# The expert stage's last normalization on other engines, its quads in one step, and one tile less

## The reference

```
h = layernorm(x) * (1 + ca) + sa
x = x + ga * attention(h)                  # 16 heads, band of 32
h = layernorm(x) * (1 + cb) + sb
y = layernorm(h + mha(h)) * g1 + be1       # 4 heads, over the 16 sequences
e = argmax(y @ Wg.T)                       # one of 8 experts per row
z = layernorm(y + relu(y @ W1[e] + b1[e]) @ W2[e] + b2[e]) * g2 + be2
out = x + gb * z
```

## Time and profile before

| What | us |
|---|---|
| median of the three timed runs | 1231.72 |
| the three runs | 1231.72, 1223.13, 1233.21 |
| profiled execution | 1211.88 |
| its span | 1210.1 |

### The profile page before, as it was taken

One profiled execution on the slowest core, in us unless ns is written; L12 is line 12 of the kernel. 1 busy time (PEld: TensorE's weight loads), 2 busy tenths in 40 slices (PEclk: granted clock), 3 DMA queues, 4 the chain that ended last, 5 costly groups with the idle time before them and its releaser, 6 DMA issues. The chain is left out here.

```text
span 1210.1 us, 51704 instructions
## 1 busy us (share of the span) xinstructions
PE 1081.4 (89%) x18513; PEld 871.2 (72%) x18513; DVE 947.0 (78%) x4152; ACT 921.3 (76%) x3404; POOL 871.5 (72%) x732
## 2 busy tenths in 40 slices
PE   4799999999999999999999999489888887788994
PEld 2578778787777778787787777258676666677883
DVE  6888888888888888888888877358775664676775
ACT  3699999999999999999999989358664644355552
POOL 2788888888888888888888857354664666555667
PEclk9899999999999999999999999789877877899998
DMA  6776777777777776776777766351331117456100
GB/s 198 205 183 172 185 172 178 186 183 179 178 177 169 182 174 170 189 181 168 185 181 175 172 172 150 92 167 41 113 105 60 56 68 207 157 166 178 54 28 30
DMA packets 111037, 181.03 MB, mean 150 GB/s; under 512 B 19726, under 2 KB 64177, under 8 KB 110656
## 3 DMA queue, kind: packets, MB, share of 16 engines
q1 hardware_dynamic: 103520, 159.32, 51.8%
q0 software_dynamic: 6400, 16.82, 3.8%
q10 hardware_dynamic: 864, 1.57, 0.5%
HBM read 35.20 MB, written 24.73 MB: 50 GB/s over the span
## 5 line engine op out<-in xcount | busy, mean ns | idle before, releaser
L621 POOL TENSOR_TENSOR qk<-mm,sw 128x1024 f32<-128x1024 f32 x128 | 305.4, 2386 | 94.6 <-DMA sw<-mm 94.4
L692 ACT ACTIVATE pr<-sm,mn 128x96 f32<-128x96 f32 x1024 | 368.4, 369 | 0.3 <-DVE mn L522 0.3
L503 DVE TENSOR_TENSOR mm<-bank,cos 128x512 f32<-128x512 f32 x256 | 175.0, 684 | 75.4 <-PE bank L325 60.6
L627 POOL TENSOR_TENSOR pr<-pr,ri 128x768 f32<-128x768 f32 x128 | 188.8, 1475 | 30.3 <-DVE ri L531 29.7
L692 ACT ACTIVATION_READ_ACCUMULATOR pr<-sm,mn 128x1 f32 x1024 | 200.4, 196 | 0.0
L522 DVE CUSTOM_DVE_ANT_0 sm<-bank,msk 128x96 f32<-128x96 f32 x1024 | 190.9, 251 | 1.7 <-PE bank L337 1.6
L504 DVE TENSOR_TENSOR mm<-bank,sin 128x512 f32<-128x512 f32 x256 | 173.9, 679 | 0.0
L702 ACT ACTIVATE pT<-bank 96x512 f32<-96x512 f32 x256 | 136.9, 585 | 16.1 <-PE bank L352 14.2
L368 PE MATMUL bank<-pT,vw 96*64 96x64 f32 x4096 | 148.9, 226 | 0.0
L1263 ACT ACTIVATE fv<-bank,b1t 128x128 f32<-128x128 f32 x288 | 81.6, 375 | 84.5 <-PE bank L1096 64.5
L368 PEld LDWEIGHTS bank<-pT,vw 96*64 96x64 f32 x4096 | 131.1, 139 | 10.2 <-issue 0.7
(11 more groups left out here) (220 smaller groups left out, 2516.7 us busy)
## 6 DMA issues: line engine op xcount, KB each, us to landing
sw<-mm SPq DMA_DIRECT2D x512, 128.0 KB, 2.4
vw<-vn SPq DMA_DIRECT2D x128, 192.0 KB, 2.6
vw<-vn SPq DMA_DIRECT2D x128, 128.0 KB, 2.4
rr<-sorted_scratch SPq DMA_DIRECT2D x72, 192.5 KB
vw<-vn SPq DMA_DIRECT2D x96, 64.0 KB, 2.6
xt<-in_x SPq DMA_DIRECT2D x16, 256.0 KB, 4.7
x_scratch<-x SPq DMA_DIRECT2D x16, 256.0 KB, 2.7
rr<-x_scratch SPq DMA_DIRECT2D x16, 256.0 KB, 3.1
```

What stands on the lines that cost most here:

```text
L503: dve.tensor_tensor(mm[s % 2][:, 0, j, :], PJ[u % 2][:, :], cos[:, :], ALU.mult)
L621: pool.tensor_tensor(qk[i % 2][:, :, 32:], mm[i % 2][:, 0, :, :], sw[i % 2][:, :, :], ALU.add)\
L627: pool.tensor_tensor(t, t, ri[i % 2][:, :].unsqueeze(2).to_broadcast([P, 8, WK]), ALU.mult)\
L692: ins = act.activation(pr[i % 2][:, h, p, :], ms_[i % 2][:, h, p, :], ACT.Exp, scale=-1.0, bias=mn[i % 2][:, h, p:p + 1], accum_out=sums[i ...
```

## The change

Third stage only.

- The root of the variance moves from GpSimd to ScalarE, as one `Sqrt` activation with the epsilon as its bias (`xnh` now holds epsilon), behind the relu of tiles 7, 11, 15 and so on. VectorE then takes the reciprocal into the new tile `xri` and scales with that. GpSimd's two instructions per quad are gone.
- VectorE's centring, gating and summing of a quad (`finish`) come in one piece at k = 1, where they were spread over k = 1 and k = 2.
- 71 tiles (`NV`) are gone through, not 72. The last quad has three tiles.
- In the last quad every tile is added, measured, rooted, scaled and scattered by itself.

```diff
+    NV = NS - 1
+    def tiles_in(q):
+        return range(min(4, NV - 4 * q))
...
-            pool.memset(xnh[:, :], -0.5).then_inc(s_rx, 1)
+            pool.memset(xnh[:, :], EPS).then_inc(s_rx, 1)
...
-            for q in range(1, NQX + 1):
-                pool.wait_ge(s_zx, q)
-                for k in range(2):
-                    scatter(q - 1, k)
-                if q < NQX:
-                    root(q)
-                for k in range(2, 4):
-                    scatter(q - 1, k)
+            for q in range(NQX):
+                for k in tiles_in(q):
+                    pool.wait_ge(s_zx, q + 1 + (k if q == NQX - 1 else 0))
+                    scatter(q, k)
...
+            def root(q, ks):
+                act.wait_ge(s_rx, 1)
+                act.wait_ge(s_sx, 4 * q + ks[-1] + 1)
+                if q >= 2:
+                    act.wait_ge(s_cx, q - 1)
+                c = slice(ks[0], ks[-1] + 1)
+                act.activation(xrs[q % 2][:, c], xmv[q % 2][:, c, 1], ACT.Sqrt, bias=xnh[:, 0:1]).then_inc(s_rx, 1)
...
                 ins.then_inc(s_hx, 1)
+                if t >= 7 and t % 4 == 3:
+                    root(t // 4 - 1, range(4))
...
-            for t in range(REST, NS):
+            for t in range(REST, NV):
                 step(t)
+            root(NQX - 2, range(4))
+            for k in tiles_in(NQX - 1):
+                root(NQX - 1, range(k, k + 1))
...
+            def finish(q, ks):
+                u, z, o, x = ux[q % 2], zx[q % 2], ox[q % 3], xs[q % NX]
+                c, n = slice(ks[0], ks[-1] + 1), q + 1 + (ks[0] if q == NQX - 1 else 0)
+                dve.wait_ge(s_rx, n + 1)
+                dve.reciprocal(xri[q % 2][:, c], xrs[q % 2][:, c]).then_inc(s_ri, 1)
...
+                for j in ks:
+                    ins = dve.tensor_scalar(z[:, j, :], u[:, j, :], xmv[q % 2][:, j, 0:1], xri[q % 2][:, j:j + 1],
+                                            ALU.subtract, ALU.mult)
+                ins.then_inc(s_cx, 1)
+                dve.wait_ge(s_cx, n)
+                dve.tensor_tensor(z[:, c, :], z[:, c, :], x[:, c, GC:GC + C], ALU.mult).then_inc(s_gx, 1)
...
+                dve.tensor_tensor(o[:, c, :], z[:, c, :], x[:, c, XC:XC + C], ALU.add).then_inc(s_zx, 1)
...
+                if k == 1 and 1 <= q <= NQX - 1:
+                    finish(q - 1, range(4))
...
+                if k == 3 and 0 <= q < NQX - 1:
+                    measure(q, range(4))
+                if q == NQX - 1 and 0 <= t < NV:
+                    measure(q, range(k, k + 1))
+                    if k:
+                        finish(q, range(k - 1, k))
...
-            for t in range(REST, NS + 7):
+            for t in range(REST, NV + 3):
                 if t < REST + 6:
                     next(second)
                 step(t)
+            finish(NQX - 1, tiles_in(NQX - 1)[-1:])
```

More of the change, by code:

```diff
@@ L879, in phase2 @@
     xrs = [sbt(p2, f"xrs{n}", [P, 4]) for n in range(2)]
+    xri = [sbt(p2, f"xri{n}", [P, 4]) for n in range(2)]
     xnh = sbt(p2, "xnh", [P, 4])
@@ L1049, in _ @@
                             bounds_check=NE * STR - 1, oob_is_err=False).then_inc(s_sca[u % 4], 16)
[L1051 to L1058 removed]
+            for q in range(NQX):
+                for k in tiles_in(q):
+                    pool.wait_ge(s_zx, q + 1 + (k if q == NQX - 1 else 0))
+                    scatter(q, k)
             for h in range(NF):
[L1060 removed]
+                pool.wait_ge(s_fin[h], sum(16 * len(tiles_in(q)) for q in range(h, NQX, NF)))
         @blk.tensor
@@ L1078, in turn @@
                 q, k = divmod(r, 2)
-                pe.wait_ge(s_xs[q % NX], 64 * (q // NX + 1))
+                pe.wait_ge(s_xs[q % NX], rows_done(q))
                 if r >= 2:
                     pe.wait_ge(s_yl, r - 1)
-                for h in range(2):
+                for h in range(min(2, NV - 2 * r)):
                     ins = pe.transpose(TY[r % 2][:, h * P:(h + 1) * P], xs[q % NX][:, 2 * k + h, 0:C], ident[:, :])
@@ L1115, in step @@
                 fetch(pe, mybir.EngineType.PE, words, t + 2)
-                if t % 2 == 0 and t + 2 < NS:
+                if t % 2 == 0 and t + 2 < NV:
                     turn(t // 2 + 1)
@@ L1238, in _ @@
                         step(t)
-            for t in range(REST, NS + 2):
+            for t in range(REST, NV + 2):
                 step(t)
@@ L1457, in _, with measure @@
             words = []
+            def measure(q, ks):
+                u, n = ux[q % 2], q + 1 + (ks[0] if q == NQX - 1 else 0)
+                c = slice(ks[0], ks[-1] + 1)
+                dve.wait_ge(s_b2b, 4 * q + ks[-1] + 1)
+                dve.wait_ge(s_yg, q + 1)
+                dve.tensor_tensor(u[:, c, :], u[:, c, :], yg[q % 2][:, c, :], ALU.add).then_inc(s_ux, 1)
+                dve.wait_ge(s_ux, n)
+                if q >= 2:
+                    dve.wait_ge(s_cx, q - 1)
+                for j in ks:
+                    ins = dve.bn_stats(xst[q % 2][:, j, :], u[:, j, :])
+                ins.then_inc(s_st, 1)
+                dve.wait_ge(s_st, n)
+                for j in ks:
+                    dve.bn_aggr(xmv[q % 2][:, j, :], xst[q % 2][:, j, :]).then_inc(s_sx, 1)
+            def finish(q, ks):
[3 more added lines that the diff above has]
+                dve.reciprocal(xri[q % 2][:, c], xrs[q % 2][:, c]).then_inc(s_ri, 1)
+                if q >= 2:
+                    dve.wait_ge(s_zx, q - 1)
+                dve.wait_ge(s_ri, NQ + n)
+                for j in ks:
+                    ins = dve.tensor_scalar(z[:, j, :], u[:, j, :], xmv[q % 2][:, j, 0:1], xri[q % 2][:, j:j + 1],
[3 more added lines that the diff above has]
+                dve.tensor_tensor(z[:, c, :], z[:, c, :], x[:, c, GC:GC + C], ALU.mult).then_inc(s_gx, 1)
+                dve.wait_ge(s_gx, n)
+                if q >= 3:
+                    dve.wait_ge(s_fin[(q - 3) % NF], 64 * ((q - 3) // NF + 1))
+                dve.tensor_tensor(o[:, c, :], z[:, c, :], x[:, c, XC:XC + C], ALU.add).then_inc(s_zx, 1)
             def low(r):
@@ L1467, in step @@
                 fetch(dve, mybir.EngineType.DVE, words, v - 2)
-                if v % 2 == 0 and v + 2 < NS:
+                if v % 2 == 0 and v + 2 < NV:
                     low(v // 2 + 1)
```

32 lines of the change are left out of this document (13 added, 19 removed).

## The result

The change made the kernel slower: ratio 1.0275 to the kernel before, 95% interval 1.019 to 1.036. The profiled execution took 1253.87 us (span 1251.7) where before it took 1211.88 (span 1210.1). The median of the four runs, 1268.33 us, holds two slow ones, which the ratio leaves out, as the ratios of the experiments leave out theirs; of the traces read here only that of e2 is of a slow run.

A forecast was written before the change was run, and what follows sets the result against it. The third stage was taken as a loop of TensorE and ScalarE, with GpSimd's root hardly in it. End -3.0 and late bias +1.0, the rest 0, gave -2.0 us on the 1231.72 median: 1229.7 us, range 1220 to 1236.

The forecast's parts named there:

- What bounds the kernel: Third stage: a loop of TensorE and ScalarE (up, relu, down), with GpSimd's root mattering only at the end.
- GpSimd's own pitch: Kernel's end: seven scatters in a row without a root, 1.27 us apart, decide the end time, not VectorE.
- The prediction's own sign of being wrong: Third stage: the stretch from tile 16 to the last `down` grows or shrinks by more than 3 us.
- None of the rivals: Four alternatives: ScalarE enters loop 1235.8 (0.16), root's neighbourhood held stage 1217.1 (0.06), end gains nothing 1231.7 (0.13), repeated loads 1273 (0.01).
- the slower one: Third stage: ScalarE enters the loop through roots, table load and late bias; +4.1 us, 1235.8; chance 0.16.
- ends on something else, which covers it: Tile 6's late bias and `down` of tile 8: hidden by ScalarE's 6.40 us idle time; 0, at most 1.5 us.
- The end: Last quad, finished by tiles with seven scatters and no GpSimd root: gain between 2.3 and 3.4 us, taken as 3.0.
- Tile 10's late bias: Start of third stage: one-piece finish makes `down` of tile 12 come 1.4 us later; +1.0, bounds 0 and 1.5.
- Table load and root on ScalarE: Third stage: one load of 1.28 us and roots of 0.22 us each delay only the high half; 0 each.
- the forecast of -2.0 us: Whole kernel: -3.0 at the end plus 1.0 for the late bias; chance 0.64.

The follow-up runs named there:

- e2: Kernel before, with GpSimd's root moved ahead of a quad's four scatters, so that four stand in a row; ratio 1.0224 to the kernel before.
- e1: Changed kernel, with an unused GpSimd add and power put back between each quad's second and third scatter; ratio 0.9999 to the kernel before.
- e9: Changed kernel, with each of a quad's four scatters waiting for one relu more (4q + 10 to 13); ratio 0.9928 to the kernel before.
- e3: Changed kernel, with centring again at the quad's second place and gate and sum at its third; ratio 1.0293 to the kernel before.
- e5: Changed kernel, with a quad's second to fourth scatter waiting for relus 4q + 10, 11 and 12; ratio 1.0103 to the kernel before.
- e12: Kernel before, with scatters spaced by relu waits as in e9 and GpSimd's root ahead of the second; ratio 1.0161 to the kernel before.
- e6: Kernel before, with second to fourth scatter each waiting for one relu more, root still ahead of the third; ratio 0.9962 to the kernel before.
- e7: Changed kernel, with each scatter writing only the first 64 of a tile's 128 rows; ratio 1.0379 to the kernel before.
- e8: Changed kernel, with every scatter row index beyond the output, so no row is written; ratio 1.0253 to the kernel before.
- e4: Changed kernel, with a quad's second to fourth scatter waiting for relus that were already done; ratio 1.0348 to the kernel before.
- e11: Kernel before, with only the second stage's scatters to the sorted scratch spread over GpSimd's next round; ratio 0.9804 to the kernel before.

## Why the prediction was wrong

The prediction said 1229.7 us, within 1%; its range of 1220 to 1236 missed. Step by step:

**What bounds the kernel: here it failed.** "So the stage is a loop of TensorE and ScalarE, up, relu, down, and GpSimd's root is hardly in it." Nobody waits for the root; that much was right. But its removal was costed only at the end, as "GpSimd's own pitch". In the other 17 quads, what the removal moves, two scatters against two others, got no term at all. e1 shows that this missing term is the loss, to within 0.5%, and e2 that it is most of it by itself. Even what ScalarE waits for TensorE before the change is in part late reports: 28 of these waits, the two on `remote` among them, end on a rise that is 0.4 to 1.9 us late, 28 us in all. The prediction's own sign of being wrong came: the stage grew by far more than 3 us, for `down` of tile 12 starts 4.2 us later than before and the last quad's first bias 44.3. None of the rivals held it either: the slower one looked at ScalarE (e1: it costs nothing that can be measured).

**The sign was in the rows.** Of the wait of 6.40 us up to 1049.99 the prediction said that it "ends on something else, which covers it". GpSimd's timeline of the kernel before names it:

```profile
1040.83 1.09 POOL L1047 DMA_INDIRECT sorted_scratch<-rr,slot  x1 [3.34 <-DVE slot L1586]
1042.22 1.07 POOL L1047 DMA_INDIRECT sorted_scratch<-rr,slot  x1 [0.30 <-issue]
1043.60 0.97 POOL L1047 DMA_INDIRECT sorted_scratch<-rr,slot  x1 [0.30 <-issue]
1044.87 1.38 POOL L1047 DMA_INDIRECT sorted_scratch<-rr,slot  x1 [0.30 <-issue]
1046.56 1.34 POOL L987 DMA_INDIRECT out<-h,rr  x1 [0.30 <-issue]
1048.20 0.97 POOL L987 DMA_INDIRECT out<-h,rr  x1 [0.30 <-issue]
```

Six scatters in a row end at 1049.17, the wait 0.82 later. An estimate from it, in proportion: four of six scatters would hold 6.40 x 4 / 6 = 4.3 us, some 70 us in 17 quads. That is an upper bound, since part of such a wait was there before; the change cost 44.

**The end was right.** -3.0 was forecast; from the first bias to the span's end the changed kernel has 2.7 less, e9 (1193.16 to 1209.0) 3.1 less than before. Seven scatters stand in a row at a pitch of (1248.89 - 1241.20) / 6 = 1.28 us, and VectorE keeps ahead of them, as the earlier trace rows let expect:

```profile
1241.20 0.97 POOL L995 DMA_INDIRECT out<-h,rr  x1 [2.36 <-DVE h L1499]
...
1248.89 0.97 POOL L995 DMA_INDIRECT out<-h,rr  x1 [0.30 <-issue]
```

**Tile 10's late bias: the mechanism was right, its size in this kernel larger.** Forecast were 1.4 us of delay for `down` of tile 12; it starts at 1064.44, 2.66 us behind its relu, which ends at 1061.78, where it was 0.14:

```profile
1062.55 0.69 DVE L1499 TENSOR_TENSOR h<-h,rr 128x512 f32<-128x512 f32 x1
...
1063.90 0.29 DVE L1522 TENSOR_TENSOR h<-bank,b2r 128x128 f32<-128x128 f32 x1
...
1064.44 1.15 PE L1103 MATMUL bank<-w,fv 128*128 x8 [1.48 <-DVE h L1522]
```

TensorE's waits for VectorE's bias from 1030 to 1080 are 5.2 us before, 6.6 in e9 and 6.8 in e1: 1.4 to 1.6 for this, where +1.0 and at most 1.5 was forecast; in the changed kernel itself they are 9.2. e3 took it away (5.4 us) and won nothing.

**Table load and root on ScalarE: right.** The rows that answer to the earlier trace rows:

```profile
1036.40 2.17 ACT L1265 ACTIVATE fv<-bank,b1t 128x128 f32<-128x128 f32 x8 [3.51 <-remote]
1038.59 1.28 ACT L1252 ACT_TABLE_LOAD   x1
1039.88 0.30 ACT L1252 ACTIVATE xrs<-xmv,xnh 128x4 f32<-128x4 f32 x1
1040.08 0.36 ACT L1244 ACTIVATE yh<-bank 128x256 bf16<-128x256 f32 x1
```

The high half starts 1.51 us behind the relu's end; 1.50 was forecast, and there is one load. An estimate by the Trainium skill's 2.66 us for a switch ("ScalarE: Activation LUTs", "What ACT_TABLE_LOAD costs") with the 0.22 of the root would be 2.9. The load starts 0.02 us behind the relu, and no drain is seen. A root takes 0.317 us where 0.22 was estimated, and waits for VectorE only in the last quad, 7.1 us in three waits.

**The whole, without the row:** e1 is the change with the scatters kept apart. 0.9999 (0.9946 to 1.0051) agrees with the forecast of -2.0 us, 0.998, and cannot tell it from nothing.

**What stays open.** How much of the 44 us is waiting and how much the lower clock that came with it: in e5 and e12 the clock is at 2.4 GHz from 1100 to 1150 and TensorE's busy time still falls from 45.15 to 41.91 and 42.32, so the waits cost without it; in the changed kernel the clock adds to them. There a `down` of eight matmuls takes 2.02 us at 1100.65, at a granted clock of 0.53, and 1.06 at 1103.42, at 1.00. Why pairs cost 1% in e5 and nothing in e1 and e6 is not shown either; in e5 a relu's report starts half of them, so that they would always meet the same part of TensorE's work, which was not tried. And what it is in a scatter that holds TensorE up is not shown: e7 and e8 rule out the data written and a cost in proportion to the rows, no more.

## What to carry to other kernels

Before an instruction is taken off an engine with time to spare, look at what it stands between: its neighbours move together, and on GpSimd a row of indirect DMAs reaches other engines. A wait that ends on `remote`, or a consumer that does two tiles' work at a stretch, is a wait to be explained before anything is hidden behind it. And when waits are put in to space work, read from a timeline that they hold; in e4 they did not, in e5 and e6 only in part, and in e12 they made a row of their own.

## What the runs showed of the hardware

GpSimd's indirect DMAs in a row, at their pitch of 1.28 us, hold back TensorE. From 1060 to 1196 us of the changed kernel, 40 of its 45 late semaphore rises come 0.6 to 1.4 us after the end of the last scatter of a row; the relus that wait for them start 0.90 and 0.82 us after it in the two places shown (1108.54 to 1109.44, 1049.17 to 1049.99). Small matmuls come out at two to four per 0.75 us until then (958.51, with the row's end at 959.09). Rows of four cost 2.2 to 3.8% here, of three 1.6%, of two from nothing to 1%, and single ones nothing that shows in the time, though the traces show one holding small matmuls (e11, 959.32). ScalarE's and VectorE's reports are not held: in the same window theirs are at most 0.02 us late. The Trainium skill, "SBUF — State Buffer", section "SBUF: two separate sides", has only VectorE and GpSimd wait for each other on the engines' side and TensorE for nobody; the runs here do not agree that TensorE goes undisturbed, though by which path it is disturbed none of them shows. It does not take the rows' data to do it: with every row index out of bounds (e8) the loss is the same, 2.5%.
